# Two graph layers on one core: eight slots for the loaded adjacency codes in place of four

## What is computed

```python
# layer 0
e0 = leaky_relu(einsum('bid,bjd->bij', x * a0, x), 0.2)
alpha = sigmoid(where(adj == 1, e0, -big))
x = layernorm(x + einsum('bij,bjd->bid', alpha, x) + bias)
# layer 1
H = x @ W;  s = H @ a_src;  d = H @ a_dst
e = where(adj != 0, exp(-leaky_relu(s[:, :, None] + d[:, None, :], 0.2)), 0)
x = layernorm(x + elu(einsum('bnm,bmo->bno', e, H) / rowsum(e)))
```

## Time and profile before

| | |
|---|---|
| median of 3 runs | 1391.45 us (1388.99 to 1396.03) |
| the profiled execution | 1394.09 us, its span 1392.4 us |
| busy: PE, DVE, ACT, POOL | 1288.6, 1020.3, 858.3, 837.5 us |
| mean granted TensorE clock | 0.982 |

### The profile page before, as it was taken

How to read it: one execution, slowest core, us unless ns; L and a number is a source line. 1 busy time by engine, 2 the same in 40 slices (tenths; PEclk the granted TensorE clock), 3 DMA queues, 4 the chain that set the end, 5 groups by cost and what they waited for, 6 DMA issues and landing times.

```text
span 1392.4 us, 27439 instructions
## 1 busy us (share of the span) xinstructions
PE 1288.6 (93%) x7874; PEld 1153.7 (83%) x7874; DVE 1020.3 (73%) x2594; ACT 858.3 (62%) x2129; POOL 837.5 (60%) x1228
## 2 busy tenths in 40 slices
PE   4898999999999999999999999999999999999996
PEld 3787888888888898888888888898888988888885
DVE  3776777777787777777777787777777777787765
ACT  3664757567584765757557584765747667584742
POOL 4554848467394755838477394755838467394732
PEclk9999999999999999999999999999999999999998
DMA  5537162351706327162441706326162351706201
GB/s 128 73 53 119 23 103 68 60 113 30 130 29 99 82 32 137 26 98 68 67 110 27 134 24 102 79 34 136 26 98 68 63 111 30 132 27 93 57 1 33
DMA packets 190352, 101.73 MB, mean 73 GB/s; under 512 B 140656, under 2 KB 173808, under 8 KB 190320
## 3 DMA queue, kind: packets, MB, share of 16 engines
q1 hardware_dynamic: 171888, 67.79, 22.3%
q0 software_dynamic: 18432, 33.56, 16.4%
HBM read 84.55 MB, written 16.78 MB: 73 GB/s over the span
## 4 chain that ended last, share of the span: by engine, by line
PE 44%; POOL 23%; DVE 18%; issue 7%; ACT 6%; DMA 1%; DVEq 1%; POOLq 0%; SPq 0%; ACTq 0%
POOL coef_lo L367 12%; PE acc_bank L1210 11%; PE hh_bank L1189 6%; PE acc_bank L1091 5%; DVE coef L868 5%; PE acc_bank L1092 5%; PE acc_bank L1093 5%; PE lg_bank L1091 3%; PE lg_bank L1093 3%; PE lg_bank L1092 3%; POOL rstd L388 3%; DVE reluP L902 2%; POOL rstd L378 2%; DVE stats L910 2%; DVE resid L905 2%
## 5 line engine op out<-in xcount | busy, mean ns | idle before, releaser
L1210 PE MATMUL acc_bank<-H,coef 128*128 128x258 f32 x2048 | 470.0, 383 | 19.5 <-ACT reluP L606 18.2
L1210 PEld LDWEIGHTS acc_bank<-H,coef 128*128 128x128 f32 x2048 | 382.2, 190 | 82.8 <-issue 28.9
L367 POOL TENSOR_TENSOR coef_lo<-coef,coef_hi 128x1024 fp32r<-128x1024 f32 x128 | 305.7, 2389 | 58.4 <-ACT coef_hi L554 57.7
L1091 PE MATMUL acc_bank<-h_hi,coef_hi 128*128 128x256 f32 x1024 | 303.4, 296 | 1.8 <-issue 1.8
L1092 PE MATMUL acc_bank<-h_lo,coef_hi 128*128 128x256 f32 x1024 | 292.2, 285 | 0.0
L1093 PE MATMUL acc_bank<-h_hi,coef_lo 128*128 128x256 f32 x1024 | 292.0, 285 | 0.0
L868 DVE SCALAR_TENSOR_TENSOR coef<-tr_bank,E_col,codeT 128x256 f32<-128x256 f32 x512 | 209.2, 476 | 38.2 <-PE acc_bank L1210 35.7
L353 POOL DMA_DIRECT2D code_nat<-in_adj x128 | 73.5, 575 | 229.5 <-DMA codeT<-code_nat 209.1
L1091 PEld LDWEIGHTS acc_bank<-h_hi,coef_hi 128*128 128x128 f32 x1024 | 199.9, 195 | 2.8 <-issue 2.0
L1092 PEld LDWEIGHTS acc_bank<-h_lo,coef_hi 128*128 128x128 f32 x1024 | 200.2, 196 | 0.0
L1093 PEld LDWEIGHTS acc_bank<-h_hi,coef_lo 128*128 128x128 f32 x1024 | 199.9, 195 | 0.0
(11 more groups left out here) (76 smaller groups left out, 2295.4 us busy)
## 6 DMA issues: line engine op xcount, KB each, us to landing
code_nat<-in_adj POOLq DMA_DIRECT2D x128, 256.0 KB, 3.7
x_raw<-in_x SPq DMA_DIRECT2D x16, 1024.0 KB, 5.6
out<-x SPq DMA_DIRECT2D x128, 128.0 KB, 1.7
codeT<-code_nat SPq DMA_TRANSPOSE x128, 3.6
W_ext<-in_L_gnn_W SPq DMA_DIRECT2D x1, 256.0 KB, 2.9
score<-in_L_gnn_a SPq DMA_DIRECT2D x1, 256.0 KB, 6.7
bias_bc<-in_L_gnn_bias SPq DMA_DIRECT2D x1, 128.0 KB, 4.0
a_col<-in_L_gnn_a SPq DMA_DIRECT2D x4, 1.0 KB, 2.2
```

The costliest lines, as they stand in the source:

```text
L367: nc.gpsimd.tensor_tensor(coef_lo[:, t % 4, :, :], blocks(coef[:, t % 4, :]), f32(coef_hi[:, t % 4, :, :]), ALU.subtract).then_inc(S.lo0, 1)
L1091: nc.tensor.matmul(dst, lhs_hi, rhs_hi, start=first, stop=False)
L1210: ins = nc.tensor.matmul(acc_bank[t % 2][:, 0:HC], coef[:, SLOT1[t], J * P:(J + 1) * P], H[:, J, :], start=J == 0, stop=J == NT - 1)
```

## The change

`code_nat` gets 8 slots in place of 4, block t in slot t, with a semaphore of its own for each slot in both directions. So a load waits only for the transposition of the same block of the graph before. All eight loads of graph b+1 are issued in steps 5 to 8 of layer 0 of graph b, two in each step; those between the layers and in layer 1 are gone. For graph 0 all eight are issued at the start, ahead of the bias and of `low_x`. The general path keeps four slots.

```diff
-        self.adj_loaded = [sem(tag + f"adj_loaded{i}") for i in range(4)]
+        self.adj_loaded = [sem(tag + f"adj_loaded{i}") for i in range(4 if general else 8)]
...
-        code_nat = sb("code_nat", [P, 4, N], BF16)
+        code_nat = sb("code_nat", [P, NT, N], BF16)
...
             def turn_codes(b, t, first):
-                sp.wait_ge(F.adj_loaded[t % 4], 32 * b + 16 * (t // 4) + 16)
+                sp.wait_ge(F.adj_loaded[t], 16 * b + 16)
...
                     if S is F:
-                        pool.wait_ge(F.codes_turned[t % 4], 32 * b + 16 * (t // 4))
+                        pool.wait_ge(F.codes_turned[t], 16 * b)
...
                     if nxt and t >= 5:
-                        load_adj(F, b + 1, t - 5, False)
+                        load_adj(F, b + 1, 2 * t - 10, False)
+                        load_adj(F, b + 1, 2 * t - 9, False)
                 if nxt:
                     next_bias(b, NT - 1)
-                    for t in range(4, 7):
-                        load_adj(F, b + 1, t, False)
+
                     low_x(F, b + 1, 0)
...
-                        if t == 2:
-                            load_adj(F, b + 1, 7, False)
+
...
-            for t in range(4):
+            for t in range(NT):
                 load_adj(F, 0, t, True)
             for t in range(NT):
                 add_bias(F, 0, t)
             for c in range(4):
                 low_x(F, 0, c)
-            for t in range(4, NT):
-                load_adj(F, 0, t, False)
+
```

More of the change, by code:

```diff
@@ L62, in __init__ @@
         else:
-            self.codes_turned = [sem(tag + f"codes_turned{i}") for i in range(4)]
+            self.codes_turned = [sem(tag + f"codes_turned{i}") for i in range(8)]
         self.mask0 = sem(tag + "mask0")
@@ L292, in turn_codes @@
                 sp.dma_start_transpose(codeT[:, t, :].rearrange("p (j i) -> p j i", i=P),
-                                       code_nat[:, t % 4, :]).then_inc(F.codes_turned[t % 4], 16)
+                                       code_nat[:, t, :]).then_inc(F.codes_turned[t], 16)
             def graph(b, loads, nxt=True):
@@ L349, in load_adj @@
                     if S is F:
-                        pool.wait_ge(F.codes_turned[t % 4], 32 * b + 16 * (t // 4))
+                        pool.wait_ge(F.codes_turned[t], 16 * b)
                     else:
                         pool.wait_ge(S.codes, NT * b + t - 3)
-                pool.dma_start(code_nat[:, t % 4, :], adj_v[b, t, :, :]).then_inc(S.adj_loaded[t % 4], 16)
+                i = t if S is F else t % 4
+                pool.dma_start(code_nat[:, i, :], adj_v[b, t, :, :]).then_inc(S.adj_loaded[i], 16)
             def low_x(S, b, c):
@@ L535, in watch_codes @@
             def watch_codes(b, t):
-                act.wait_ge(F.codes_turned[t % 4], 32 * b + 16 * (t // 4) + 16)
+                act.wait_ge(F.codes_turned[t], 16 * b + 16)
                 if t == 0 and not (isinstance(b, int) and b == 0):
@@ L786, in mask0_below @@
                 dve.wait_ge(F.tanh, NT * b + t + 1)
-                dve.wait_ge(F.codes_turned[t % 4], 32 * b + 16 * (t // 4) + 16)
+                dve.wait_ge(F.codes_turned[t], 16 * b + 16)
                 if t >= 4:
```

## The result

| | before | after |
|---|---|---|
| median of nine runs each, alternated on one chip | 1392.01 us (1388.99 to 1396.03) | 1383.78 us (1381.46 to 1385.5) |
| the profiled execution, its span | 1394.09, 1392.4 us | 1382.85, 1381.2 us |
| mean granted TensorE clock | 0.982 | 0.984 |

The ratio is 0.9937, with a 95% interval of 0.9922 to 0.9951: a small gain, but clear of the noise. It is 8 us in the medians and 11.2 us between the two profiled executions.

The account below looks back on a forecast made before the run. It took a chain of engines handing work on in fixed order (PE 44%, POOL 23%, DVE 18%) as the bound; −8.4 and −2.15 us made −10.55, giving 1383.5 or 1380.9 us, middle 1382 us, range 1377.5 to 1388.5.

Parts of the forecast that it names:

- L902 meets L358: DVE's L902 stands behind POOL's h_lo row, 3.24 us of it in graph 0; the change removes it, −8.4 us.
- Rival 1: Only graph 0 gains; the other graphs' stalls, 5.2 us, return as another wait: 1386 us, chance 0.13.
- Rival 2: Nothing changes, POOL's 209 us were idle time of an engine with slack: 1391.5 us, chance 0.08.
- Graph 0's clock: PE's low clock after 3.81 us of idleness in graph 0 goes with the stall: −2.15 us.
- The short falls of the clock: Falls of 3.4 us length elsewhere, each costing PE at most half; two more or fewer make 3 us.
- What L358 meets in its new place: Beside the earlier h_lo, DVE's L868 is no slower and L778 ends 0.28 us ahead: cost 0.
- rival 3: L778 meets the earlier L358 and waits 2.5 us, 37 us in 15 graphs: 1418 us; chance 0.05 together with the blocked-loads rival.
- Four more loads: POOL's added loads in steps 5 to 8 of layer 0 fit, 0.24 us to spare in step 6: taken as 0.
- Rival 4: Added loads are blocked by DVE, one per graph costing 34 us: 1416 us; chance 0.05 together with the L778 rival.
- Start, transpositions, stores: Eight loads at the start put POOL 2.32 us later, with 10 us of cover; earlier transpositions and stores gain nothing: 0.
- The sum: −10.55 us: 1383.5 us from the profiled execution, 1380.9 us from the median; the middle, 1382 us, was taken.
- The rule and the row: Literal rule: graph 0's L902 waits some 0.9 us for one L358, sum 2.3 us smaller; the row's longer wait was used.

Follow-up runs that it names:

- Order alone: Kernel before with its four slots, only the loads of blocks 4 to 6 moved behind the last h_lo: 1384.33 us, ratio 0.9958.
- slots alone: Changed kernel with its eight slots, the loads of blocks 4 to 7 put back in their old places: 1384.65 us, ratio 0.9965.
- one late h_lo: Changed kernel with only the fourth low_x held until mask1 is done, in each graph: 1392.32 us, ratio 1.0009.
- all four late: Changed kernel with POOL's four low_x held until mask1 is done, just ahead of L901: 1417.68 us, ratio 1.0207.
- L902 in the second of four: Changed kernel with POOL's four low_x held until ACT's second L516 of row 3, so L902 arrives in the second: 1417.27 us, ratio 1.019.

## Why the prediction was right, by its steps

**L902 meets L358 (−8.4 us).** Right in mechanism and size: 62.4 to 53.6 us is −8.8. Order alone and slots alone both remove it and both give the gain; one late h_lo brings 8.8 us of it back and costs 7.1 to 8.3. Rival 1 (the stalls of the other graphs return as another wait) is thereby out: 13 graphs behind graph 0 lost 5.2 us, against the 5.2 us that the prediction gave them. Rival 2 (nothing changes) is out with it.

**Graph 0's clock (−2.15 us).** Graph 0 became 5.67 us shorter, of which L902 is 3.25, leaving 2.4. With a stall of that size in each graph, the same difference came out as 2.1 us per graph. Both are differences, not a separate measurement of the clock's price.

**The short falls of the clock (0 in the sum, ±3 us in the range).** They did not stay as they were: the trace of before has eight of some 3.4 us behind graph 0, at places like the 322.3 us of the earlier trace rows, that of the changed kernel ten. The prediction's bound of half of 3.4 us for each was safe. At that place a fall costs less than that: from one graph's first L901 to the next's, a graph of the changed kernel with one takes 83.06 to 83.37 us, a graph without 82.73 to 82.89, so some 0.4 us each. By this estimate the two more falls took back about 0.8 us.

**What L358 meets in its new place (0).** Right. Timeline of graph 6, against the earlier trace rows:

```profile
598.89 0.15 DVE L777 TENSOR_TENSOR watch_max<-watch_max,watch_sum 128x8 f32<-128x8 f32 x1
599.43 2.51 POOL L359 TENSOR_TENSOR h_lo<-x_raw,h_hi 128x512 fp32r<-128x512 f32 x2 [7.78 <-ACT h_hi L502]
...
603.97 2.51 POOL L359 TENSOR_TENSOR h_lo<-x_raw,h_hi 128x512 fp32r<-128x512 f32 x2 [2.03 <-ACT h_hi L502]
```

L777 ends at 599.04, 0.39 us ahead of the first h_lo, and 0.39 to 0.41 us in all 15 graphs; rival 3 did not occur. L901 follows at 610.41, 3.9 us behind the last h_lo (4 us predicted).

**Four more loads (0, with 0.24 us left in step 6).** Graph 7's step 6, against the earlier trace rows:

```profile
661.05 1.13 POOL L354 DMA_DIRECT2D code_nat<-in_adj  x2
662.48 0.19 POOL L376 TENSOR_TENSOR var_eps<-moments,eps_col 128x1 f32<-128x1 f32 x1 [0.29 <-DVE moments L829]
```

0.29 us left; in one graph of the 15 (graph 13) only 0.02. The pair took 1.13 us, and with each load split in two there was still no cost that can be told, so the true margin is wider than this wait. Rival 4 is out: no load was held up.

**Start, transpositions, stores (0).** POOL's start, against the earlier trace rows:

```profile
13.63 4.44 POOL L354 DMA_DIRECT2D code_nat<-in_adj  x8 [11.63 <-DMA x_raw<-in_x]
...
48.53 10.17 POOL L368 TENSOR_TENSOR coef_lo<-coef,coef_hi 128x1024 fp32r<-128x1024 f32 x4 [20.05 <-ACT coef_hi L553]
```

Eight loads in a row, 4.44 us, and the first coef_lo still waits 20 us for ACT.

**The sum.** Against its own profiled execution it was −10.55 forecast and −11.24 measured. Against the medians it was −9.5 forecast (1391.45 to 1382.0) and −8.2 measured. What the prediction took too large there is, as far as two executions can tell, the size of the stall in a usual run: it read it from one execution, in which L902 stood 8.8 us over its undisturbed sum, while another had 4.6. The prediction's remark that the spread of the runs before "may be these very stalls" fits that. The kernel before spread over 7 us in these nine runs and over 12.6 us in 23 others, the changed one over 4 us. The step from 1383.5 down to the middle at 1382 leaned on the median and was the wrong way. An execution above the median probably had more of the stalls (this rests on the two that were profiled), and the kernel without them ends at the same place whatever it started from.

**The rule and the row.** The prediction set the Trainium skill ("SBUF — State Buffer", section "Who interferes with whom") against graph 0: by the rule DVE should wait for one POOL instruction, and the row showed it waiting to the end of the fourth. I went by the row, which was right for this kernel. But the rule fits where no load stands directly ahead of the row (0.58 to 0.98 us of waiting, in all graphs of the kernels with all four late and with L902 in the second of four), and where I had taken the row for a law, in the expectation for the kernel with all four late, I came out at twice to nearly three times the 34 us measured.

## What to carry to other kernels

An engine's idle wait can be costly although nobody waits for that engine, because it moves the next work on top of something else: look at what runs beside the work that is released, not only at who waits for it. Before adding buffers to end such a wait, try moving the waiting instruction behind the work that needs nothing; here that gave the same gain for no memory. And where one stall of a kind is found, list every DVE line whose mean is above its minimum: L837's stalls behind xb were nearly three times those of L902, and the order that removes them was 13.5 us faster again.

## What the runs showed of the hardware

- A DVE instruction with two SBUF operands that meets a row of POOL TENSOR_TENSOR instructions gets in when the current one ends: 1.00 and 1.05 us in place of 0.42, in each of the 15 graphs of two kernels. When the row directly follows a DMA that POOL issued, DVE stays out to the end of the row: 3.97 us with four h_lo, 6.16 us with eight xb (there a TENSOR_SCALAR). One pair of kernels tests this nearly alone (1417.27 against 1469.22 us; the release also differs by one count). Why a load ahead makes the difference was not found, nor whether it has to be directly ahead.
- The norm's TENSOR_SCALAR (L836) is stalled by POOL's xb as well: 0.78 to 0.80 us on average in four of eight row blocks with an xb behind the rstd, 0.41 us where the xb wait until it is done.
- After 3.81 to 3.97 us without a matmul TensorE's granted clock was 0.51 and 0.50, the 1.2 GHz level, and what the graph lost beyond the stall itself was 2.1 to 2.4 us, more than half of the stall. After 1.98 us without one it fell to 0.50 in every second graph, and 32 matmuls took 8.89 us in place of 7.43; in the graphs between it stayed at 1.00 there.
